# Probabilities times v of an attention group: one block of PE work instead of two

## The reference

```python
x = layer_norm(hidden, ln1); q, k, v = split(x @ c_attn_w + c_attn_b)
hidden = hidden + merge(attn(q, k, v, causal)) @ attn_proj_w + attn_proj_b
x = layer_norm(hidden, lnx); q = x @ q_attn_w + q_attn_b
k, v = split(ctx @ x_kv_w + x_kv_b)
hidden = hidden + merge(attn(q, k, v, scorer_logits, tril k=2)) @ x_proj_w + x_proj_b
x = layer_norm(hidden, ln2)
out = hidden + gelu(x @ fc_w + fc_b) @ mlp_proj_w + mlp_proj_b
```

## Time and profile before

| what | value |
|---|---|
| median of 3 runs | 1208.4 us (1208.26 to 1210.92) |
| the profiled execution | 1205.04 us |
| its span, from first to last instruction | 1203.3 us |
| PE busy | 1089.1 us, 91% of the span |
| DVE, ACT, POOL busy | 792.5, 612.3, 441.2 us |
| PE busy from 95 to 1140 us, where the attentions run | 985.33 of 1045 us |
| mean granted TensorE clock | 0.977 |

### The profile page before, as it was taken

One profiled execution on the slowest core, in us unless ns is written; L12 is line 12 of the kernel. 1 busy time (PEld: TensorE's weight loads), 2 busy tenths in 40 slices (PEclk: granted clock), 3 DMA queues, 4 the chain that ended last, 5 costly groups with the idle time before them and its releaser, 6 DMA issues.

```text
span 1203.3 us, 20614 instructions
## 1 busy us (share of the span) xinstructions
PE 1089.1 (91%) x7360; PEld 654.3 (54%) x7360; DVE 792.5 (66%) x1898; ACT 612.3 (51%) x1154; POOL 441.2 (37%) x805
## 2 busy tenths in 40 slices
PE   5659889899999999999999999999899999898877
PEld 2335546464556545674466645675466645464444
DVE  3448667777866777667876777767876677565223
ACT  1126455556644565545654575545744465455413
POOL 3204443435443523435343433435442342324220
PEclk9769999999999999999999999999999999999989
DMA  8951256271434535262254526253354412400000
GB/s 234 137 91 29 50 79 101 43 98 28 68 53 68 71 56 87 37 89 45 48 72 63 76 38 90 50 72 50 57 76 63 58 28 49 59 14 2 9 9 18
DMA packets 53528, 74.16 MB, mean 62 GB/s; under 512 B 9571, under 2 KB 27939, under 8 KB 53412
## 3 DMA queue, kind: packets, MB, share of 16 engines
q1 hardware_dynamic: 53428, 72.86, 39.1%
HBM read 17.45 MB, written 4.19 MB: 18 GB/s over the span
## 4 chain that ended last, share of the span: by engine, by line
PE 67%; DVE 12%; ACT 8%; issue 5%; DMA 4%; SPq 4%; POOL 2%; DVEq 0%; ACTq 0%; POOLq 0%
PE dense L536 16%; PE dense L530 14%; PE pv_out L608 11%; PE scores L594 8%; PE max_scores L574 8%; DVE row_max L810 4%; PE max_scores L577 3%; PE dense L524 3%; SPq L501 3%; DMA q_stack<-parts_q 2%; ACT inner L725 2%; ACT probs L699 1%; DMA q_stack<-max_rows 1%; PE dense L631 1%; DVE rest_k L843 1%
## 5 line engine op out<-in xcount | busy, mean ns | idle before, releaser
L699 ACT ACTIVATE probs<-scores 128x512 f32<-128x512 f32 (+3 forms) x768 | 383.4, 529 | 338.0 <-PE scores L594 334.0
L810 DVE TENSOR_REDUCE row_max<-max_scores 128x1 f32<-128x512 f32 (+6 forms) x1024 | 443.8, 481 | 138.7 <-PE max_scores L577 137.2
L968 POOL TENSOR_SCALAR_AFFINE_SELECT probs<-probs 128x256 f32<-128x256 f32 x512 | 215.6, 440 | 513.2 <-ACT probs L699 513.0
L574 PE MATMUL max_scores<-k_stack,q_stack 96*128 96x512 bf16 (+7 forms) x1024 | 284.5, 304 | 19.1 <-DVE row_max L810 15.1
L594 PE MATMUL scores<-q_stack,k_stack 98*128 98x512 bf16 (+7 forms) x1024 | 266.3, 301 | 32.8 <-ACT probs L699 17.7
L608 PE MATMUL pv_out<-probs,v_ones 128*32 128x512 f32 (+6 forms) x2048 | 166.5, 442 | 0.0
L574 PEld LDWEIGHTS max_scores<-k_stack,q_stack 96*128 96x128 bf16 (+1 forms) x1024 | 100.4, 98 | 95.5 <-issue 45.2
L594 PEld LDWEIGHTS scores<-q_stack,k_stack 98*128 98x128 bf16 (+1 forms) x1024 | 89.5, 98 | 97.4 <-ACT probs L699 28.7
L536 PE MATMUL dense<-mlp_w,inner 128*128 128x256 f32 x512 | 122.3, 385 | 9.4 <-DVE rest_k L843 4.2
L530 PE MATMUL dense<-feat_b,fc_w 128*128 128x512 f32 x256 | 125.0, 615 | 2.5 <-ACT rest_k L734 1.1
L536 PEld LDWEIGHTS dense<-mlp_w,inner 128*128 128x128 f32 x512 | 94.1, 190 | 29.3 <-DVE rest_k L843 5.4
(11 more groups left out here) (87 smaller groups left out, 1251.2 us busy)
## 6 DMA issues: line engine op xcount, KB each, us to landing
q_stack<-parts_q SPq DMA_DIRECT2D x192, 128.0 KB, 4.9
k_stack<-parts_k SPq DMA_DIRECT2D x192, 128.0 KB, 5.3
x_in<-in_x SPq DMA_DIRECT2D x8, 512.0 KB, 8.4
x_in<-in_ctx SPq DMA_DIRECT2D x8, 512.0 KB, 8.0
hidden<-in_x SPq DMA_DIRECT2D x8, 512.0 KB, 6.3
out_y<-hidden SPq DMA_DIRECT2D x32, 128.0 KB, 1.7
fc_w<-in_w_fc SPq DMA_DIRECT2D x1, 1024.0 KB, 10.1
mlp_w<-in_w_mlp SPq DMA_DIRECT2D x1, 1024.0 KB, 14.7
```

The source lines that it names most:

```text
L574: pe.matmul(max_scores[:, bank, c0:c0 + W[q]], queries[0:rows_, head, q * P:(q + 1) * P], keys[0:rows_, head, 0:W[q]], start=True, stop=False)
L699: nc.scalar.activation(probs[:, head % (2 * GH), c0:c0 + w], scores[:, part % EXP_BANKS, 0:w], ACT.Exp, scale=SCALE).then_inc(exp_done, 1)
L810: last = nc.vector.tensor_reduce(row_max[:, g % 2, c:c + 1], max_scores[:, part % MAX_BANKS, c0:c0 + W[q]], AX.X, ALU.max)
L968: nc.gpsimd.affine_select(out=v, in_=v, compare_op=ALU.is_ge, fill=0.0, base=q0 - kb * P + LAST[at.kind], pattern=[[0, 2], [1, P]], channe ...
```

## The change

The table that says at which beat of twelve the key blocks of PV run has one entry instead of two: all four at beat 5. Nothing else changes. PE's PV items of a group then stand one behind the other, behind M and S of beat 5 and ahead of the plan of that beat. ACT's copy of pv_out, which stands with the last PV item, moves from beat 7 to beat 5. MT stays at beat 7 and ON at beat 10.

```diff
-PV_AT, ON_AT, MT_AFTER = {4: (0, 1), 7: (2, 3)}, 10, 2
+PV_AT, ON_AT, MT_AFTER = {5: (0, 1, 2, 3)}, 10, 2
```

## The result

The change makes the kernel slower: 1218.1 us (median of 4 runs, 1217.4 to 1219.6) against 1208.3 (4 runs, 1208.1 to 1210.9), ratio 1.0078, 95% interval 1.006 to 1.0095. The forecast was 1208.2, 1200 to 1214.5.

A forecast was written before the change was run, and what follows sets the result against it. PE was taken to bound the kernel (busy 91%, 67% of the chain). Saved switches were spent on lost covers: -1.5 - 1.5 - 1.33 + 2.6 + 0.9 + 1.0 = 0.2 us faster, 1208.2 us, range 1200 to 1214.5.

The forecast's parts named there:

- X41: Last group of an X stage: f.5 loses the second block's cover while ACT empties banks; loss 1.18 us a pass.
- Y5: First group of a Y stage: DVE's CAST starts ahead of POOL's R1, MT stops waiting; gain 1.20 us a pass.
- The rival that kept it behind R1: Maxima at Y5 stay behind POOL's R1, so Y5 gains nothing: 1214.2 us, chance 0.15.
- X17: Second group of an X stage: p2.1 comes later, POOL's R2 and then t2.1 move with it; loss 0.65 us a pass.
- Y17 and Y29: Two Y-stage groups: p1.1 and q2.0 come 0.65 us later, delaying k2.1 and q2.1; loss 0.32 us together a pass.
- the 17 groups left: Groups at the start and end not followed place by place: put at +1.0 us gain, bounds +4.2 and -4.
- the tx place: First full X stage, with a twin near the end: the second block runs inside tx.0's wait; gain 1.3 us each.
- M at X30: First full X stage: M waits 2.58 us for a DMA with the second block behind it; gain 0.9 us.
- X5 of iteration 2: No dense work covers DVE's layer norm statistics there: a loss of 1.25 us in place of a 0.25 gain.
- All off the end: Rival: all 15.9 us of saved PE switch time shortens the run, 1192.5 us; chance 0.12.
- X41 taken up: Rival: later PE waits at X46 and Y3 absorb the loss at X41, giving 1201.1 us; chance 0.18.
- Masks: Rival: PV waits for POOL's masks, needed two beats earlier; 0.1 us a group gives 1214.6 us; chance 0.05.

The follow-up runs named there:

- e9: Changed kernel with two result-discarding matmuls ahead of each of six TensorE waits in iterations 1, 2 and 7: 1212.3 us (before 1209.0; ratio 1.0027).
- e10: Kernel before the change with result-discarding matmuls ahead of its waits, three at tx.0 (twice) and M at X30, one at M of Y25: 1201.7 us (0.9944).
- e11: Against the kernel before: one block only at X5, X29, Y5 and two places where tx.0 waits, plus wait-filling matmuls: 1196.0 us (0.9878).
- e12: As e11, but two blocks at the two places where tx.0 waits, and three wait-filling matmuls there: 1193.2 us (0.987).
- e3: Changed kernel with two blocks again at X41's group in iterations 2 to 7: 1211.7 us (1.0011).
- e16: Against the kernel before: one block only at X5 (iterations 3 to 7), X29 (2 to 7), Y5 (2 to 6), no added matmuls: 1199.5 us against 1209.0.
- e5: Changed kernel with four result-discarding matmuls ahead of each of six TensorE waits in iterations 1, 2 and 7: 1213.0 us (before 1208.3; ratio 1.005).

## Why the prediction was wrong

**The mechanism of the pass held, step by step.** X41, after:

```profile
583.74 0.33 PE L594 MATMUL scores<-q_stack,k_stack 98*128 98x384 bf16 x1
...
585.03 0.34 PE L594 MATMUL scores<-q_stack,k_stack 98*128 98x256 bf16 x2 [0.67 <-ACT probs L699]
585.30 2.37 PE L608 MATMUL pv_out<-probs,v_ones 128*32 128x512 f32 x32
587.60 1.98 PE L530 MATMUL dense<-feat_b,fc_w 128*128 128x512 f32 x4
...
590.94 1.55 PE L530 MATMUL dense<-feat_b,fc_w 128*128 128x512 f32 x3 [0.41 <-ACT rest_k L734]
```

From S of X40, f.4 starts 3.86 later (foreseen 3.83, before 2.36) and f.5 7.20 (foreseen 7.14, before 5.97). Y5, after:

```profile
603.90 0.17 DVE L819 CAST max_parts<-row_max 128x16 bf16<-128x16 f32 x1
...
605.66 2.36 POOL L913 TENSOR_TENSOR hidden<-hidden,row 128x1024 f32<-128x1024 f32 x1
...
606.42 0.22 PE L627 MATMUL dense<-ident_b,max_parts 128*128 128x128 bf16 x1
```

The CAST comes 1.76 ahead of R1 and takes 0.17, not 1.76; MT has no wait and comes 4.09 behind S of Y4 (602.33; foreseen 4.11, before 5.33). The rival that kept it behind R1 is out. X17, after:

```profile
559.10 2.36 POOL L913 TENSOR_TENSOR hold<-hidden,row 128x1024 f32<-128x1024 f32 x1
...
559.89 1.85 DVE L847 CAST parts_q<-rest_q 128x512 bf16<-128x512 f32 x1
...
562.33 0.28 PE L574 MATMUL max_scores<-k_stack,q_stack 96*128 96x256 bf16 x1 [1.03 <-DVE row_max L810]
...
566.60 0.65 PE L524 MATMUL dense<-ident,normed 128*128 128x128 f32 x4 [0.94 <-DVE rest_k L843]
```

t2.1 stays 7.50 behind R2's start, as in the earlier trace rows, and so moves with R2. But its own wait did not grow, as I had listed: the new one is at M of X26, one item earlier on DVE's queue. X5 and X29 gain 0.24 and 0.27.

**Sizes in the pass.** Measured 0.70 a pass, forecast 0.30. Half of the difference is Y17 and Y29. Y29, after:

```profile
643.66 0.75 DVE L843 SCALAR_TENSOR_TENSOR rest_q<-dense,col,parts_q 128x512 f32<-128x512 f32 x1 [3.99 <-ACT parts_q L721]
```

```profile
644.47 1.98 PE L530 MATMUL dense<-feat_b,q_w 128*128 128x512 f32 x4
```

q2.1 follows the rest by 0.75 + 0.06, as assumed, but I had added it up wrongly: from the earlier trace rows, 633.86 + 0.65 + 0.06 = 634.57, a loss of 0.27, not of 0.16. The steps are 0.31 at Y29 and 0.23 at Y17, 0.54 for 0.32. The others: Y5 gains 1.07 and not 1.20, Y41 0.08 and not 0.15, since an S behind PV waits about 0.1 for an exponential that now stands behind ACT's copy in more groups than the one I saw this in. Over five passes these sizes make 2.0 of the 9.9 between forecast and result.

**The step that failed is the term of "the 17 groups left".** Ahead of the passes the prediction had the tx place (+1.3), M at X30 (+0.9), X5 of iteration 2 (-1.25 in its place) and nine of the 17 groups (X17 to X41 of iteration 0; X5, X41 and Y5 to Y41 of iteration 1), which were put at +1.0 in all with bounds of +4.2 and -4; together a gain of about 1.5. The table shows a loss of 6.8 (5.5 in e9 against e10).

The first two terms came, as a sum: from X7 to X31 the changed kernel gains 2.30, where 2.2 were foreseen. From tx.0 to tx.1 it takes 2.87 and not 4.21, 1.34 less:

```profile
150.58 0.30 PE L524 MATMUL dense<-ident,normed 128*128 128x128 f32 x1 [2.15 <-POOL normed L928]
...
153.45 1.12 PE L524 MATMUL dense<-ident,normed 128*128 128x128 f32 x4
```

But that was priced with a block at half the clock: with both kernels' waits filled the two terms make 1.36 (e9 against e10), and the tx place alone 0.32 (e11 against e12). At X30 the block did go into the DMA wait, where M waits 2.02 and not 2.58. At the end the same gain is 1.94 from Y7 to Y19 of iteration 7, and 2.49 are lost from Y19 to Y31, with the clock at its lower level from 1040 to 1047 us; in e9 against e10 it is 0.76 and stays. X5 of iteration 2 came too: Y43 to X7 loses 1.50.

The loss is in the nine groups. X19 to X7, with X5 of iteration 1, loses 3.2 (1.7 in e9 against e10), and Y19 to Y31, with Y29, loses 3.35 (0.66). X5 of iteration 1 has no dense work ahead, as that of iteration 2; I had not followed it, though the earlier trace rows had shown me the pattern. M waits 1.75 there, TensorE falls to its lower level, and the PV block takes 3.40 (2.37 in e9, in which the wait is filled). M at Y25 waits 1.80 and not 1.48, and here too TensorE is at its lower level behind the wait, from 224 to 231 us, where before it was at 1.00:

```profile
126.08 3.40 PE L608 MATMUL pv_out<-probs,v_ones 128*32 128x512 f32 x32
...
223.63 0.38 PE L574 MATMUL max_scores<-k_stack,q_stack 99*128 99x386 bf16 x1 [1.80 <-DVE row_max L810]
```

The bounds were too narrow because I took the worst of the 17 groups at a place with covers from the pass, and because none of them held the clock that falls behind a wait. At the start dense work is thin, and a block was the cover itself. The end lost 0.6 to 1.3.

**The rivals.** All off the end: out, the saving is spent. X41 taken up: out (e3). Masks: PV's loads wait for them more often, but the first matmul of a block never starts more than 0.31 us after the start of the matmul ahead of it in the changed kernel's trace (0.15 in 61 of 64 groups), so these waits lie within the way in: out. None of the rivals came; what came is the forecast's own mechanism, spent covers, at the places that I had followed least, and behind the longer waits the lower clock, to a share that is open.

## What to carry to other kernels

A short block between two long ones is often a cover: before it is merged away, list which engine's chain ends behind it, place by place, and keep the split where one does. Here three places of eight gained more than 0.2 us, and a kernel that joins only those is 0.7% faster where joining all was 0.8% slower. Follow the start and the end of a pipeline by the same rows as its steady part, and price no place from a row at half the clock. Before the clock is blamed for a difference, give both kernels the same cure, and look whether both are cured: it helped both here, and one of them still had stretches at the lower level.

## What the runs showed of the hardware

Matmuls that do nothing but fill waits are worth something: ten of them took the kernel before from 1209.0 to 1201.7 (e10), and with twenty, eight of them in the tail, e16's choice went from 1199.5 to 1193.2 (e12).

One DVE instruction can lose to POOL several times in a row. In the profiled execution of e5 (1219.1 us, 6 over that kernel's median):

```profile
835.80 3.69 DVE L866 CAST parts_q<-rest_q 128x512 bf16<-128x512 f32 x1
```

```profile
835.00 2.36 POOL L932 TENSOR_TENSOR hold<-hidden,row 128x1024 f32<-128x1024 f32 x1
837.31 1.16 POOL L977 TENSOR_TENSOR parts_q<-rest_q,parts_q 128x512 bf16<-128x512 f32 x1
838.41 0.79 POOL L987 TENSOR_SCALAR_AFFINE_SELECT probs<-probs 128x256 f32<-128x256 f32 x2
```

```profile
840.07 0.40 PE L591 MATMUL max_scores<-k_stack,q_stack 96*128 96x256 bf16 x1 [2.86 <-DVE row_max L829]
```

At the same place of the pass shown above (559.89) the CAST took 1.85 behind R2; here it came behind the two POOL instructions that follow R2 as well, 3.69. M waited 2.86 for DVE, TensorE went to its lower level, and this pass took 141.9 us where the others of that trace took 138.1. The Trainium skill, SBUF — State Buffer, section Who interferes with whom, says that whoever issues first holds the port pair that DVE and POOL share, and the other blocks until it is done. The 1.85 agrees; the 3.69 shows more, that the one that waits is not always the next. Such a flip may be part of the scatter of these kernels; one profiled execution does not show that.
